# Normalising the attention output: psO copied out before the reciprocal, and the reciprocal moved by a DMA

## The chip, the cores and the metric

The kernel runs on the 8 cores of one Trainium2 chip. Every core computes one of the 8 sequences, by the same program, and the cores exchange nothing. The metric is the device time of the slowest core, in microseconds. All rows below are those of core 3, the slowest one of the profiled execution.

## The reference

One transformer layer over x of [8, 2048, 1024] in float32: causal attention of 16 heads of width 64 on the normalised x, with a residual, and then a gated feed-forward part on the normalised sum, with a residual.

```python
h = layernorm(x)
q, k, v = rope(split_heads(h @ Wq)), rope(split_heads(h @ Wk)), split_heads(h @ Wv)
attn = softmax(where(causal, q @ k.T * 64 ** -0.5, -inf))
x = x + merge_heads(attn @ v) @ Wo + bo
h = layernorm(x)                      # hp: h one position earlier
r = sigmoid((mu_r * h + (1 - mu_r) * hp) @ W_r.T)
k = square(relu((mu_k * h + (1 - mu_k) * hp) @ W_k.T))
out = x + r * (k @ W_v.T)
```

## The kernel before

The program is one list of operations, each with an engine, the tokens it reads and the tokens it writes. From the tokens the helper class `_Sched` (L37) works out which earlier operations each one waits for, by one counting semaphore for each engine and one for each engine's DMA queue. Each engine then executes its own operations strictly in the order of the list. A DMA waits for the one before it on its queue too (L115 to L119), unless both are of one batch. The DMA queue "sync" is SP's, the queue "sp" is POOL's.

The stages: layer norm of x with a transpose into h1t (to 88 us), the projections of Q and K with the rotation (to 215), the projection of V and the attention (216 to 656), the product with Wo and the second layer norm (658 to 756), and the feed-forward part (to the end).

The attention takes the heads in pairs: p = 0 to 7, one head on partitions 0 to 63 of qt and kt, the other on 64 to 127. Each pair has four units ic = 0 to 3, of 512 query columns each (L457). Unit ic walks over the 4ic + 4 blocks J of 128 keys that causality leaves, so the units have 4, 8, 12 and 16 steps. In a step TensorE computes the scores of both heads (L474 and L479, into psA or psB, with the mask added by L485 and L488 on the diagonal blocks), ScalarE takes exp (L491, into one of three tiles er), and TensorE accumulates in psO: L505 adds V times er to partitions 0 to 63, L513 adds ones times er, the row sums, to partitions 64 to 127. Columns 0 to 511 are the first head's, columns 512 to 1023 the second's. The even units accumulate in psO0, the odd ones in psO1. Each has a token for each half: `otokA` and `otokB`.

A unit's tail (`tail_maker`, L522) is what VectorE does when all steps of a unit are done: the reciprocal of the 64x1024 row sums into denl (L523), the product for the first head into ao (L526, called nmA), the product for the second head into aotmp (L531, nmB), and an SP DMA of 64 KB that brings aotmp to partitions 64 to 127 of ao (L534, amv). ao, which shares its memory with h1t, is what the Wo stage reads.

The loop of L555 writes the order: the scores run one step ahead of the product with V, and the tail of a unit is put in after the first scores of the next one, ahead of its first product with V. A unit's first L505 waits for the tail of the unit two before it, which used the same psO. In pair 0 each new unit is preceded by the projection of V for four more token tiles (`emit_vproj`, L344: TensorE L352 into the four halves of psA and psB, VectorE L359 evacuates them), and these evacuations stand ahead of the preceding unit's tail on VectorE.

Wo is loaded by POOL once the scores of pair 3 are done (L571), followed on the same queue by 14 tiles of x of 512 KB each (L577). The last two tiles of x go into the memory of the tiles er and are loaded after the last step. The Wo stage (L598) waits for the last amv.

Of the kernel before, what the change touches and what calls it, by code (L numbers as in the profile page):

```python
# [158 lines left out]
def _build_nc(upto=99, taps=()):  # L159
# [37 lines left out]
    B_ao = sb("ao", [128, 16384], BF16, 86016)  # L197
# [29 lines left out]
    DENl = sb("denl", [128, 1024], F32, 218048)  # L227
    qrawK = sb("qrawK", [128, 2048], BF16, 222144)
    aotmp = sb("aotmp", [128, 1024], BF16, 226240)
# [12 lines left out]
    A = s.add  # L242
# [29 lines left out]
    for cb in range(CC):  # L272
        e, f, rd, wr = wload(WA, 1024 * cb, wq_t, 128 * cb, f"waq{cb}")
        A("sp", f, reads=rd, writes=wr, is_dma=True, name=f"ld_wq{cb}", batch="wq")
    for cb in range(CC):
        e, f, rd, wr = wload(WB, 1024 * cb, wk_t, 128 * cb, f"wbk{cb}")
# [89 lines left out]
    for j in range(TT):  # L366
# [3 lines left out]
          writes=[f"xring{j % 4}"], is_dma=True, name=f"ldx{j}", batch=f"x{j // 2}")  # L370
# [56 lines left out]
    for cb in range(CC):  # L427
        A("sp", (lambda cb=cb: lambda g: g.dma_start(WA[:, 1024 * cb:1024 * (cb + 1)],
                                                     wv_t[128 * cb:128 * (cb + 1), :]))(),
          reads=[], writes=[f"wav{cb}", f"waq{cb}"], is_dma=True, name=f"ld_wv{cb}", batch="wv")  # L430
# [29 lines left out]
    def unit_ctx(p, ic):  # L460
            psO = psO0 if ic % 2 == 0 else psO1
            otokA = "ps4" if ic % 2 == 0 else "ps6"
            otokB = "ps5" if ic % 2 == 0 else "ps7"
            nJ = 4 * ic + 4

            def emit_scores(J, slot):
                i0 = max(512 * ic, 128 * J)
                w = 512 * (ic + 1) - i0
                sreg = psA if J % 2 == 0 else psB
                stokA = "ps0" if J % 2 == 0 else "ps2"  # L470
                stokB = "ps1" if J % 2 == 0 else "ps3"
                es, etok = Er[slot], f"E{slot}"
                diag = J >= 4 * ic
                A("pe", (lambda p=p, J=J, i0=i0, w=w, sreg=sreg, diag=diag: lambda t: t.matmul(  # L474
                    sreg[:, 0:w], D_kt[0:64, 2048 * p + 128 * J:2048 * p + 128 * J + 128],
                    C_qt[0:64, 2048 * p + i0:2048 * p + i0 + w], start=True, stop=not diag,
                    tile_position=(0, 0)))(),
                  reads=[f"kt_p{p}", f"qt_p{p}"], writes=[stokA, f"qt_r{p}", f"kt_r{p}"], name=f"sA{p}_{ic}_{J}")
                A("pe", (lambda p=p, J=J, i0=i0, w=w, sreg=sreg, diag=diag: lambda t: t.matmul(  # L479
                    sreg[:, 512:512 + w], D_kt[64:128, 2048 * p + 128 * J:2048 * p + 128 * J + 128],  # L480
                    C_qt[64:128, 2048 * p + i0:2048 * p + i0 + w], start=True, stop=not diag,
                    tile_position=(64, 0)))(),
                  reads=[f"kt_p{p}", f"qt_p{p}"], writes=[stokB, f"qt_r{p}", f"kt_r{p}"], name=f"sB{p}_{ic}_{J}")
                if diag:
                    A("pe", (lambda sreg=sreg: lambda t: t.matmul(  # L485
                        sreg[:, 0:128], idb[:, :], mnegb[:, :], start=False, stop=True))(),
                      reads=["idb", "mnegb"], writes=[stokA], name=f"mA{p}_{ic}_{J}")
                    A("pe", (lambda sreg=sreg: lambda t: t.matmul(  # L488
                        sreg[:, 512:640], idb[:, :], mnegb[:, :], start=False, stop=True))(),
                      reads=["idb", "mnegb"], writes=[stokB], name=f"mB{p}_{ic}_{J}")  # L490
                A("act", (lambda sreg=sreg, es=es, w=w: lambda sc: sc.activation(  # L491
                    es[:, :].rearrange("p (a b) -> p a b", a=2)[:, :, 0:w],
                    sreg[:, :].rearrange("p (a b) -> p a b", a=2)[:, :, 0:w],
                    AF.Exp, scale=0.125))(),
                  reads=[stokA, stokB], writes=[etok, stokA, stokB], name=f"ex{p}_{ic}_{J}")

            def emit_pv(J, slot):
                i0 = max(512 * ic, 128 * J)
                w = 512 * (ic + 1) - i0
                rel = i0 - 512 * ic  # L500
                es, etok = Er[slot], f"E{slot}"
                for hb, otok, ecol, ocol in ((0, otokA, 0, 0), (1, otokB, 512, 512)):
                    h = 2 * p + hb
                    A("pe", (lambda J=J, h=h, w=w, rel=rel, es=es, ecol=ecol, ocol=ocol, psO=psO, nJ=nJ:
                             lambda t: t.matmul(  # L505
                        psO[0:64, ocol + rel:ocol + rel + w],
                        E_v[:, 1024 * J + 64 * h:1024 * J + 64 * h + 64],
                        es[:, ecol:ecol + w],
                        start=(J == 0), stop=(J == nJ - 1), tile_position=(0, 0),
                        skip_group_check=True))(),  # L510
                      reads=[etok, f"vsb{J}"], writes=[otok], name=f"pv{p}_{ic}_{J}_{hb}")
                    A("pe", (lambda J=J, w=w, rel=rel, es=es, ecol=ecol, ocol=ocol, psO=psO, nJ=nJ:
                             lambda t: t.matmul(  # L513
                        psO[64:128, ocol + rel:ocol + rel + w],
                        ones128[:, 0:64],
                        es[:, ecol:ecol + w],
                        start=(J == 0), stop=(J == nJ - 1), tile_position=(0, 64),
                        skip_group_check=True))(),
                      reads=[etok, "ones"], writes=[otok], name=f"pd{p}_{ic}_{J}_{hb}")


            def tail_maker(p=p, ic=ic, psO=psO, otokA=otokA, otokB=otokB):  # L522
                A("dve", (lambda psO=psO: lambda v: v.reciprocal(  # L523
                    DENl[64:128, :], psO[64:128, :]))(),
                  reads=[otokA, otokB], writes=["denl"], name=f"rcp{p}_{ic}")
                A("dve", (lambda p=p, ic=ic, psO=psO: lambda v: v.tensor_mul(  # L526
                    B_ao[0:64, 2048 * p + 512 * ic:2048 * p + 512 * ic + 512],
                    psO[0:64, 0:512], DENl[64:128, 0:512]))(),
                  reads=[otokA, "denl", "h1t"], writes=["ao"], name=f"nmA{p}_{ic}")
                at_sl = slice(512 * (ic % 2), 512 * (ic % 2) + 512)  # L530
                A("dve", (lambda p=p, ic=ic, psO=psO, at_sl=at_sl: lambda v: v.tensor_mul(  # L531
                    aotmp[0:64, at_sl], psO[0:64, 512:1024], DENl[64:128, 512:1024]))(),
                  reads=[otokB, "denl"], writes=[f"aot{ic % 2}", otokB], name=f"nmB{p}_{ic}")
                A("sync", (lambda p=p, ic=ic, at_sl=at_sl: lambda sy: sy.dma_start(  # L534
                    B_ao[64:128, 2048 * p + 512 * ic:2048 * p + 512 * ic + 512],
                    aotmp[0:64, at_sl]))(),
                  reads=[f"aot{ic % 2}"], writes=["ao"], is_dma=True, name=f"amv{p}_{ic}")
            return emit_scores, emit_pv, tail_maker
# [31 lines left out]
    for cb in range(CC):  # L570
        A("sp", (lambda cb=cb: lambda g: g.dma_start(Wo_sb[:, 1024 * cb:1024 * (cb + 1)],  # L571
                                                     wo_t[128 * cb:128 * (cb + 1), :]))(),
          reads=["kt_r0", "kt_r1", "kt_r2", "kt_r3"],
          writes=[f"wo{cb}"], is_dma=True, name=f"ld_wo{cb}", batch="wo")

    for j in list(range(0, 4)) + list(range(6, 16)) + [4, 5]:
        A("sp", (lambda j=j: lambda g: g.dma_start(Ax[:, 1024 * j:1024 * (j + 1)],  # L577
                                                   x_t[128 * j:128 * (j + 1), :]))(),
          reads=[], writes=[f"xt{j}"] + x_deps[j], is_dma=True, name=f"ldx2_{j}",
# [4 lines left out]
      reads=["bo32"], writes=["bo32"], is_dma=True, name="bo_ld")  # L584
    A("dve", lambda v: v.tensor_copy(boHi[0:64, :], bo32[0:64, :]),
      reads=["bo32"], writes=["bohi"], name="bo_hi")
    A("dve", lambda v: v.tensor_sub(boLo[0:64, :], bo32[0:64, :], boHi[0:64, :]),
      reads=["bo32", "bohi"], writes=["bolo"], name="bo_lo")
# [4 lines left out]
    for n, tt in enumerate(tt_order):  # L593
        for half in range(2):
            slot = halfbanks[(n * 2 + half) % 4]
            ptok = f"ps{(n * 2 + half) % 4}"
            for cb in range(CC):
# [5 lines left out]
                  reads=["ao", f"wo{cb}"], writes=[ptok, "wodone"], name=f"wo{tt}_{half}_{cb}")  # L603
# [3 lines left out]
              reads=["bohi", "ones"], writes=[ptok], name=f"bh{tt}_{half}")  # L607
# [3 lines left out]
              reads=["bolo", "ones"], writes=[ptok], name=f"bl{tt}_{half}")  # L611
# [4 lines left out]
              reads=[ptok, f"xt{tt}", f"res{tt}"], writes=[f"res{tt}", ptok], name=f"ra{tt}_{half}")  # L616
# [28 lines left out]
    for cb in range(CC):  # L645
# [3 lines left out]
          reads=["wodone"],  # L649
          writes=[f"wr{cb}"], is_dma=True, name=f"ld_wr{cb}", batch="wr")  # L650
# [39 lines left out]
    for tt in [12, 13, 14, 15, 8, 9, 10, 11, 4, 5, 6, 7, 0, 1, 2, 3]:  # L690
        for half in range(2):
            slot = halfbanks[(tt * 2 + half) % 8]
            ptok = f"ps{(tt * 2 + half) % 8}"
            for cb in range(CC):
# [5 lines left out]
                  reads=[f"xr_t{tt // 4}", f"wr{cb}"], writes=[ptok, "rmdone"], name=f"rm{tt}_{half}_{cb}")  # L700
# [3 lines left out]
              reads=[ptok, "vsb"], writes=[f"rs_t{tt}", ptok], name=f"sg{tt}_{half}")  # L704
# [3 lines left out]
    for cb in range(CC):  # L708
# [3 lines left out]
          reads=["rmdone"],  # L712
          writes=[f"wkf{cb}"], is_dma=True, name=f"ld_wkt{cb}", batch="wkt")
# [39 lines left out]
    for cb in range(CC):  # L753
# [3 lines left out]
          reads=["xkr0", "xkr1"] + [f"xr_t{t}" for t in range(4)],  # L757
          writes=[f"wvf{cb}"], is_dma=True, name=f"ld_wvt{cb}", batch="wvt")

    n_store = 0  # L760
    for tt in [12, 13, 14, 15, 8, 9, 10, 11, 4, 5, 6, 7, 0, 1, 2, 3]:
        for half in range(2):
            slot = halfbanks[(tt * 2 + half) % 8]
            ptok = f"ps{(tt * 2 + half) % 8}"
            for dk in range(CC):
# [5 lines left out]
                  reads=[f"ka_t{tt // 4}", f"wvf{dk}"], writes=[ptok], name=f"vm{tt}_{half}_{dk}")  # L771
# [3 lines left out]
              reads=[ptok, f"rs_t{tt}"], writes=["p9scr", ptok], name=f"v1{tt}_{half}")  # L775
# [81 lines left out]
```

How the kernel before makes its waits and increments, by code:

```python
            def body(eng):  # L129
                for op in per_eng[eng_name]:
                    for pkey in sorted(op.resolved_waits):
                        val = op.resolved_waits[pkey]
                        if marks.get((eng_name, pkey), 0) >= val:
                            continue
                        marks[(eng_name, pkey)] = val
                        eng.wait_ge(sems[pkey], val)
                    ins = op.fn(eng)
                    if op.is_dma:
                        ins.then_inc(sems[self.semkey(op)], 16)
                    elif op.inc_needed:
                        ins.then_inc(sems[self.semkey(op)], 1)
# [661 lines left out]
        def syb(sy):  # L803
            bodies["sync"](sy)
            for k in sorted(qtot):
                sy.wait_ge(sems[k], qtot[k])
```

## Time and profile before

| | us |
|---|---|
| median of 2 runs | 969.9 (969.31 to 970.49) |
| the profiled execution, its own time | 971.39 |
| its span, slowest core | 969.8 |
| spans of the 8 cores | 958.3 to 969.8 |
| busy in the span: PE, DVE, ACT | 754.9, 579.2, 435.9 |
| mean granted TensorE clock, core 3 | 0.941 |

The span runs from the first to the last instruction on the core; the execution's own time has something around it. PE is TensorE's matmul, PEld its weight load, DVE is VectorE, ACT ScalarE, POOL GpSimd. A busy share is an average over stages with different limits.

### The profile page before, as it was taken

What the parts mean: (1) busy time and instruction counts of PE and PEld (TensorE: products, weight loads), DVE (VectorE), ACT (ScalarE), POOL (GpSimd) and SP (SyncE); (2) the same over time, 40 slices, a digit from 0 to 9 for tenths busy, and PEclk for the clock granted to TensorE, in tenths of its full rate; (3) what the DMA queues carried; (4) which work ended last, traced back from release to release, by engine and by line L of the source; (5) the groups of instructions that cost most, each with busy time, mean ns of one, the idle gap of its engine ahead of it and who ended that gap; (6) DMA issues with size and microseconds to landing.
All of it is one profiled execution on the core that took longest, in us unless ns stands there. A gap on an engine that the chain in (4) does not pass through costs nothing.

```text
span 969.8 us, 12954 instructions; the slowest of 8 cores (958.3 to 969.8 us)
## 1 busy us (share of the span) xinstructions
PE 754.9 (78%) x4288; PEld 299.5 (31%) x4288; DVE 579.2 (60%) x740; ACT 435.9 (45%) x580; POOL 42.9 (4%) x83
## 2 busy tenths in 40 slices
PE   0115999969998787878787877768998499297998
PEld 0113444423332222222222222212343244043443
DVE  3554443563545848484848575754777886056587
ACT  3444332311246676767676767651444233022200
POOL 3100001000000000001300000000001000101000
PEclk9999999999999898989998999996999699598999
DMA  7960337320000000000860000010000500600633
GB/s 172 190 174 31 77 77 130 88 65 1 4 4 3 9 5 9 4 9 14 164 228 9 4 9 4 9 32 18 1 1 8 80 1 1 87 1 4 127 152 152
DMA packets 21121, 52.30 MB, mean 54 GB/s; under 512 B 3360, under 2 KB 5408, under 8 KB 21056
## 3 DMA queue, kind: packets, MB, share of 16 engines
q0 software_dynamic: 10816, 24.20, 13.4%
q1 hardware_dynamic: 8704, 23.07, 7.7%
q10 hardware_dynamic: 1536, 4.20, 1.9%
q8 instruction: 36, 0.59, 0.2%
q14 instruction: 29, 0.24, 0.1%
HBM read 47.26 MB, written 8.39 MB: 57 GB/s over the span
## 4 chain that ended last, share of the span: by engine, by line
PE 54%; DVE 15%; ACT 14%; DMA 11%; issue 5%; POOL 1%; DVEq 0%; ACTq 0%; SPq 0%; POOLq 0%
ACT er L491 11%; PE psO L505 11%; DVE denl L523 5%; DMA xri<-x 5%; PE psO L402 5%; PE psA L474 5%; PE psO L766 3%; PE psA L352 3%; PE psB L598 3%; PE psB L352 2%; PE psA L402 2%; PE psA L598 2%; DMA swp<-qraw 2%; PE psB L402 2%; DVE xr L669 2%
## 5 line engine op out<-in xcount | busy, mean ns | idle before, releaser
L523 DVE RECIPROCAL denl<-psO 64x1024 f32<-64x1024 f32 x32 | 209.9, 6560 | 119.3 <-PE psO L513 118.5
L505 PE MATMUL psO<-er,vsb 128*64 128x512 bf16 (+3 forms) x640 | 181.7, 364 | 74.8 <-ACT er L491 49.9
L491 ACT ACTIVATE er<-psA 128x1024 bf16<-128x1024 f32 (+1 forms) x160 | 150.2, 939 | 132.0 <-PE psA L479 96.2
L513 PE MATMUL psO<-er,ones 128*64 128x512 bf16 (+3 forms) x640 | 187.4, 374 | 0.0
L491 ACT ACTIVATE er<-psB 128x1024 bf16<-128x1024 f32 (+2 forms) x160 | 136.0, 850 | 11.9 <-PE psB L488 8.0
L505 PEld LDWEIGHTS psO<-er,vsb 128*64 128x64 bf16 x640 | 47.7, 108 | 144.6 <-issue 138.1
L320 PE MATMUL psO<-idb,hs 128*128 128x128 bf16 x128 | 16.2, 307 | 72.4 <-ACT hs L305 70.0
L479 PE MATMUL psA<-qt,kt 64*128 64x512 bf16 (+1 forms) x160 | 61.0, 381 | 0.0
L474 PE MATMUL psA<-qt,kt 64*128 64x512 bf16 (+1 forms) x160 | 61.0, 381 | 0.0
L418 DVE TENSOR_TENSOR swp<-swp,sinb 128x2048 bf16<-128x2048 bf16 x16 | 19.6, 1225 | 67.2 <-DMA swp<-qraw 57.7
L479 PE MATMUL psB<-qt,kt 64*128 64x512 bf16 (+2 forms) x160 | 56.4, 353 | 0.3
L474 PE MATMUL psB<-qt,kt 64*128 64x512 bf16 (+2 forms) x160 | 56.5, 353 | 0.0
L737 DVE TENSOR_TENSOR ka<-ka 128x512 bf16<-128x512 bf16 x32 | 13.6, 425 | 56.7 <-ACT ka L733 56.6
L513 PEld LDWEIGHTS psO<-er,ones 128*64 128x64 bf16 x640 | 46.9, 109 | 0.0
L598 PE MATMUL psA<-wosb,ao 128*128 128x512 bf16 x128 | 33.7, 411 | 10.3 <-DMA ao<-aotmp 10.3
L721 PE MATMUL psA<-xkr,wktsb 128*128 128x512 bf16 x64 | 18.7, 458 | 25.1 <-DMA wktsb<-wkt 18.9
L352 PE MATMUL psA<-wa,h1t 128*128 128x512 bf16 x128 | 31.0, 399 | 8.0 <-DVE vsb L359 8.0
L410 ACT CAST qraw<-psO 128x512 bf16<-128x512 f32 x32 | 18.8, 586 | 38.8 <-PE psO L402 17.1
L286 ACT ACTIVATE vsb<-ax 128x1024 bf16<-128x1024 f32 x16 | 16.9, 1057 | 42.8 <-DVE ax L612 42.8
L282 DVE TENSOR_REDUCE stats<-xri 128x1 f32<-128x1024 f32 x16 | 19.4, 1213 | 27.6 <-DMA xri<-x 27.6
L320 PEld LDWEIGHTS psO<-idb,hs 128*128 128x128 bf16 x128 | 12.4, 138 | 75.9 <-issue 75.9
L474 PEld LDWEIGHTS psA<-qt,kt 64*128 64x128 bf16 x160 | 14.9, 93 | 60.1 <-issue 60.1
(129 smaller groups left out, 1192.3 us busy)
## 6 DMA issues: line engine op xcount, KB each, us to landing
xri<-x SPq DMA_DIRECT2D x16, 512.0 KB, 6.4
ax<-x POOLq DMA_DIRECT2D x16, 512.0 KB, 12.9
out<-ax SPq DMA_DIRECT2D x16, 512.0 KB, 2.6
swp<-qraw ACTq DMA_DIRECT2D x24, 128.0 KB, 2.4
swp<-qraw SPq DMA_DIRECT2D x24, 128.0 KB, 2.7
wa<-wq POOLq DMA_DIRECT2D x8, 256.0 KB, 12.9
wb<-wk POOLq DMA_DIRECT2D x8, 256.0 KB, 13.1
wa<-wv POOLq DMA_DIRECT2D x8, 256.0 KB, 11.2
```

The source lines that it names most:

```text
L320: return t.matmul(o, h_ap_fn(k), idb[:, :], start=(k4 == 0), stop=(k4 == 3), is_transpose=True)
L352: return t.matmul(ps[:, o:o + 512], B_h1t[:, 2048 * cb + 128 * tt:2048 * cb + 128 * tt + 128], WA[:, 1024 * cb + 512 * half:1024 * cb + 51 ...
L402: return t.matmul(ps[:, o:o + 512], Wsb[:, 1024 * cb + 128 * co:1024 * cb + 128 * co + 128], B_h1t[:, 2048 * cb + 512 * tch:2048 * cb + 51 ...
L418: A("dve", (lambda sw=sw: lambda v: v.tensor_mul(sw[:, :], sw[:, :], sinb[:, :]))(), reads=stoks + ["sinb"], writes=stoks, name=f"{tag}r1_ ...
L474: A("pe", (lambda p=p, J=J, i0=i0, w=w, sreg=sreg, diag=diag: lambda t: t.matmul(sreg[:, 0:w], D_kt[0:64, 2048 * p + 128 * J:2048 * p + 12 ...
L479: A("pe", (lambda p=p, J=J, i0=i0, w=w, sreg=sreg, diag=diag: lambda t: t.matmul(sreg[:, 512:512 + w], D_kt[64:128, 2048 * p + 128 * J:204 ...
L491: A("act", (lambda sreg=sreg, es=es, w=w: lambda sc: sc.activation(es[:, :].rearrange("p (a b) -> p a b", a=2)[:, :, 0:w], sreg[:, :].rear ...
L505: lambda t: t.matmul(psO[0:64, ocol + rel:ocol + rel + w], E_v[:, 1024 * J + 64 * h:1024 * J + 64 * h + 64], es[:, ecol:ecol + w], start=( ...
L513: lambda t: t.matmul(psO[64:128, ocol + rel:ocol + rel + w], ones128[:, 0:64], es[:, ecol:ecol + w], start=(J == 0), stop=(J == nJ - 1), t ...
L523: A("dve", (lambda psO=psO: lambda v: v.reciprocal(DENl[64:128, :], psO[64:128, :]))(), reads=[otokA, otokB], writes=["denl"], name=f"rcp{ ...
L598: A("pe", (lambda tt=tt, half=half, cb=cb, slot=slot: lambda t: t.matmul(slot[0][:, slot[1]:slot[1] + 512], B_ao[:, 2048 * cb + 128 * tt:2 ...
L766: A("pe", (lambda tt=tt, half=half, dk=dk, slot=slot: lambda t: t.matmul(slot[0][:, slot[1]:slot[1] + 512], B_ka[:, 2048 * dk + 128 * tt:2 ...
```

## The change

In the tail of a unit, the row sums, the first head's part of psO and the second head's part are first copied to SBUF by VectorE: denl in float32, ao and aotmp in bfloat16. The reciprocal then reads and writes denl in SBUF, partitions 64 to 127. A new SP DMA (dmv) moves the 64x1024 reciprocals, 256 KB of float32, to partitions 0 to 63 of denl, and the two products are done in place in SBUF, with both operands on partitions 0 to 63. The DMA of aotmp into ao follows as before. Nothing else is changed.

```diff
             def tail_maker(p=p, ic=ic, psO=psO, otokA=otokA, otokB=otokB):
-                A("dve", (lambda psO=psO: lambda v: v.reciprocal(
+                at_sl = slice(512 * (ic % 2), 512 * (ic % 2) + 512)
+                A("dve", (lambda psO=psO: lambda v: v.tensor_copy(
                     DENl[64:128, :], psO[64:128, :]))(),
-                  reads=[otokA, otokB], writes=["denl"], name=f"rcp{p}_{ic}")
-                A("dve", (lambda p=p, ic=ic, psO=psO: lambda v: v.tensor_mul(
+                  reads=[otokA, otokB], writes=["denl", otokA, otokB], name=f"cpD{p}_{ic}")
+                A("dve", (lambda p=p, ic=ic, psO=psO: lambda v: v.tensor_copy(
                     B_ao[0:64, 2048 * p + 512 * ic:2048 * p + 512 * ic + 512],
-                    psO[0:64, 0:512], DENl[64:128, 0:512]))(),
-                  reads=[otokA, "denl", "h1t"], writes=["ao"], name=f"nmA{p}_{ic}")
-                at_sl = slice(512 * (ic % 2), 512 * (ic % 2) + 512)
-                A("dve", (lambda p=p, ic=ic, psO=psO, at_sl=at_sl: lambda v: v.tensor_mul(
-                    aotmp[0:64, at_sl], psO[0:64, 512:1024], DENl[64:128, 512:1024]))(),
-                  reads=[otokB, "denl"], writes=[f"aot{ic % 2}", otokB], name=f"nmB{p}_{ic}")
+                    psO[0:64, 0:512]))(),
+                  reads=[otokA, "h1t"], writes=["aoU", otokA], name=f"cpOA{p}_{ic}")
+                A("dve", (lambda psO=psO, at_sl=at_sl: lambda v: v.tensor_copy(
+                    aotmp[0:64, at_sl], psO[0:64, 512:1024]))(),
+                  reads=[otokB], writes=[f"aot{ic % 2}", otokB], name=f"cpOB{p}_{ic}")
+                A("dve", lambda v: v.reciprocal(DENl[64:128, :], DENl[64:128, :]),
+                  reads=["denl"], writes=["denl"], name=f"rcp{p}_{ic}")
+                A("sync", lambda sy: sy.dma_start(DENl[0:64, :], DENl[64:128, :]),
+                  reads=["denl"], writes=["denl2"], is_dma=True, name=f"dmv{p}_{ic}")
+                A("dve", (lambda p=p, ic=ic: lambda v: v.tensor_mul(
+                    B_ao[0:64, 2048 * p + 512 * ic:2048 * p + 512 * ic + 512],
+                    B_ao[0:64, 2048 * p + 512 * ic:2048 * p + 512 * ic + 512],
+                    DENl[0:64, 0:512]))(),
+                  reads=["aoU", "denl2"], writes=["ao"], name=f"nmA{p}_{ic}")
+                A("dve", (lambda ic=ic, at_sl=at_sl: lambda v: v.tensor_mul(
+                    aotmp[0:64, at_sl], aotmp[0:64, at_sl], DENl[0:64, 512:1024]))(),
+                  reads=[f"aot{ic % 2}", "denl2"], writes=[f"aot{ic % 2}"], name=f"nmB{p}_{ic}")
```

## Rows read from the trace of the kernel before

**Rows 1.** The page, part 4: the chain that ended last, by line.
```profile
ACT er L491 11%; PE psO L505 11%; DVE denl L523 5%; DMA xri<-x 5%; PE psO L402 5%; PE psA L474 5%; PE psO L766 3%; PE psA L352 3%; PE psB L598 3%; PE psB L352 2%; PE psA L402 2%; PE psA L598 2%; DMA swp<-qraw 2%; PE psB L402 2%; DVE xr L669 2%
```

**Rows 2.** Stretches of pairs 1 and 4: busy us by engine, clock, DMA share, GB/s.
```profile
312.00:361.00 49.00, 39.60 (x282) 13.00 (x282) 31.36 (x12) 34.80 (x42) 0.00 (x0) 0.93 0.03 7
457.50:505.00 47.50, 37.71 (x274) 12.52 (x272) 31.36 (x12) 34.40 (x41) 10.61 (x21) 0.96 0.81 206
```

**Rows 3.** VectorE in order of time, pair 1: start, us; idle before, releaser.
```profile
312.92 6.56 DVE L523 RECIPROCAL denl<-psO 64x1024 f32<-64x1024 f32 x1 [9.63 <-PE psO L513]
319.65 0.68 DVE L526 TENSOR_TENSOR ao<-psO,denl 64x512 bf16<-64x512 f32 x1 [0.17 <-DVE denl L523]
320.26 0.67 DVE L531 TENSOR_TENSOR aotmp<-psO,denl 64x512 bf16<-64x512 f32 x1
321.10 6.56 DVE L523 RECIPROCAL denl<-psO 64x1024 f32<-64x1024 f32 x1 [0.17 <-PE psO L513]
...
330.01 6.56 DVE L523 RECIPROCAL denl<-psO 64x1024 f32<-64x1024 f32 x1 [0.90 <-PE psO L513]
...
343.18 6.56 DVE L523 RECIPROCAL denl<-psO 64x1024 f32<-64x1024 f32 x1 [5.16 <-PE psO L513]
...
361.06 6.56 DVE L523 RECIPROCAL denl<-psO 64x1024 f32<-64x1024 f32 x1 [9.49 <-PE psO L513]
```

**Rows 4.** TensorE in order of time around the start of unit 1, pair 1.
```profile
313.91 0.38 PE L505 MATMUL psO<-er,vsb 128*64 128x512 bf16 x1 [0.65 <-ACT er L491]
...
316.54 0.22 PE L505 MATMUL psO<-er,vsb 128*64 128x128 bf16 x1
...
320.48 0.61 PE L505 MATMUL psO<-er,vsb 128*64 128x512 bf16 x1 [3.39 <-DVE ao L526]
```

**Rows 5.** Waits of TensorE for VectorE (us, times, longest), and all reciprocals.
```profile
PE psO L505 <- DVE ao L526: 23.7, 7, 3.4
...
L523 DVE RECIPROCAL denl<-psO x32: 6560/6560/6562, 245.5 to 648.3; 64x1024 f32<-64x1024 f32 x32
```

**Rows 6.** Short stretches, columns as in rows 2: the granted clock.
```profile
320.00:321.00 1.00, 0.52 (x2) 0.16 (x2) 0.93 (x2) 0.00 (x0) 0.00 (x0) 0.50 0.00 0
325.00:326.00 1.00, 1.00 (x6) 0.32 (x6) 1.00 (x1) 0.25 (x1) 0.00 (x0) 0.50 0.00 0
326.00:327.00 1.00, 1.00 (x10) 0.27 (x8) 1.00 (x1) 0.78 (x1) 0.00 (x0) 0.86 0.00 0
656.00:658.00 2.00, 0.00 (x0) 0.00 (x0) 1.24 (x2) 0.00 (x0) 0.00 (x0) 0.50 0.14 32
```

**Rows 7.** The chain in order of time in pair 0: start us, us, what.
```profile
246.28 0.38 PE psO L505
...
253.25 3.56 PE psA L352 x16
256.81 3.45 PE psB L352 x16
```

**Rows 8.** VectorE's groups by shape: busy, mean ns, idle before and releasers.
```profile
L776 DVE TENSOR_TENSOR ax<-ax,dscr 128x512 f32<-128x512 f32 x32 | 22.2, 692 | 3.3
L526 DVE TENSOR_TENSOR ao<-psO,denl 64x512 bf16<-64x512 f32 x32 | 21.8, 683 | 6.9 <-DVE denl L523 5.6 <-DMA ao<-aotmp 1.2
...
L359 DVE CAST vsb<-psA 128x512 bf16<-128x512 f32 x16 | 11.1, 691 | 26.9 <-PE psA L352 26.7 <-DVE vsb L359 0.2
...
L587 DVE TENSOR_TENSOR bolo<-bo,bohi 64x1024 bf16<-64x1024 f32 x1 | 1.2, 1216 | 0.1
...
L585 DVE CAST bohi<-bo 64x1024 bf16<-64x1024 f32 x1 | 0.7, 685 | 2.4 <-DMA bo<-bo 2.4
```

**Rows 9.** The chain in order of time at the end of the attention.
```profile
648.32 6.57 DVE denl L523
...
655.73 0.61 DVE aotmp L531
...
656.46 1.90 DMA ao<-aotmp
658.36 0.14 issue
658.50 1.86 PE psA L598 x4
```

**Rows 10.** DMA issues: KB each, median us from issue to landing.
```profile
out<-ax SPq DMA_DIRECT2D x16, 512.0 KB, 2.6
swp<-qraw ACTq DMA_DIRECT2D x24, 128.0 KB, 2.4
...
ao<-aotmp SPq DMA_DIRECT2D x32, 64.0 KB, 1.9
```

**Rows 11.** Landing of the single L534 DMA issued in 464:467, 480:484 and 490:496.
```profile
DMA to landing us min/median/max: 7.7/7.7/7.7
...
DMA to landing us min/median/max: 7.0/7.0/7.0
...
DMA to landing us min/median/max: 5.5/5.5/5.5
```

## The prediction

> **What bounds the kernel now.** I read the page's chain first [rows 1]: the two attention lines L491 (exp) and L505 (the product with V) are the longest terms, and the reciprocal at L523 is third with 5%. Then the stretches [rows 2]: one pair of heads takes 47.5 to 48.5 us from the second pair on, TensorE is busy about 38 us of it and VectorE 31.4, so no engine is full on average; the granted clock is 0.93 to 0.96. The question is which wait ends last where a unit begins. VectorE's order of time shows a tail [rows 3]: the reciprocal at 312.92, nmA at 319.65, nmB at 320.26, next reciprocal at 321.10, 8.18 us. The reciprocals of units 0, 1, 2 and 3 of the pair start at 321.10, 330.01, 343.18 and 361.06. That of unit 0 is late: its last product was issued at 316.54 [rows 4], and VectorE was still in the tail of the preceding unit 3. TensorE meanwhile stands before unit 1, because psO1 is read by that same tail: its product at 320.48 came 3.39 us late, released by nmA (L526) [rows 4]. This happens once per pair: 7 times, 23.7 us in all [rows 5]. After the idle time the granted clock is at 0.50, which is the 1.2 GHz level, and returns to 1.00 (2.4 GHz) at about 326 [rows 6]: unit 1 then needs 9.5 us (320.48 to 330.01), where the same eight steps of pair 0 took 7.0 us at full clock (246.28 to 253.25) [rows 7].
>
> **What the change takes away.** psO is freed once three copies have read it, and not after the reciprocal. Count from the tail's start. cpD, 64x1024 from PSUM: 128x512 casts from PSUM take 0.69 us, 64x1024 at one element per cycle takes 1.22 (L587) [rows 8], so 1.22 (the ends are 0.69 and 1.23). cpOA waits for it through a semaphore, 0.17 as between L523 and L526 [rows 3], and takes 0.69, as L359 [rows 8]. So psO's first half is free at 2.1 us, where it was 7.4. In the pair read above the stall of 3.4 us would shrink to the wait for exp, about 0.5 to 1 us (the step without a stall at 313.91 shows 0.65 [rows 4]), and the slow clock's 2.5 us would go too. About 2.7 + 2.5 = 5.2 us per pair, 36 us over seven, if nothing else became late.
>
> **What it adds: a longer tail on VectorE, one instruction stream.** VectorE takes its instructions in order, and nmA now waits for the DMA dmv. Behind nmA on VectorE stand nmB and the next unit's cpD, cpOA and cpOB, and for these TensorE waits. So the DMA's landing time counts as VectorE time. The length D of a tail, start to start:
> cpD 1.22, gap 0.17, cpOA 0.61 (start to start, as nmA to nmB [rows 3]), cpOB 0.69, together 2.69. Then the reciprocal 6.56, now from SBUF: 6.4 ns per element is far over one cycle, so the division sets it and not the source, and I keep it: 9.25. Issue and landing of dmv: 0.12 from nmB's end to the DMA and 0.14 from its landing to the waiting engine, both from the end of the attention stage [rows 9], around a landing time X. Then nmA 0.61 and nmB 0.67. D = 9.25 + 0.26 + X + 1.28 = 10.8 + X. In the SBUF form of nmA a 128x512 tensor_tensor of float32 takes 0.69 (L776) [rows 8], so it is no cheaper and no dearer.
> X is for 256 KB in 64 pieces of 4 KB. Rows: 64 KB in pieces of 1 KB land in 1.9, 128 KB in pieces of 4 KB in 2.4 (with a second such transfer beside it), 512 KB of 128 pieces in 2.6 [rows 10]. I take 2.6, the upper neighbour. The ends are 1.9 and 3.4 (0.5 more for each 64 KB, as between the first two). D is 13.4, from 12.7 to 14.2.
>
> **Does D bind?** Four tails take 4 x 13.4 = 53.6 us, and a pair now takes 48. The other limit is TensorE's: tail 0 cannot start before tail 3's end (D after it), unit 2 needs psO0 from tail 0 (2.1 later), then units 2 and 3 run 13.2 + 17.9 = 31.1 us [rows 3], plus up to 2.5 for a slow clock. That is D + 33.2 to D + 35.7, 49.1 at most with D at 13.4. It passes 4D only below D = 11.9. So from the tail of unit 3 of pair 0 (312.92), with VectorE idle before it, every later tail finds its unit ready and they follow one another without a pause. Check at the tightest place: unit 3 starts 2.1 after tail 1's start, or when unit 2 ends, and its own tail comes 2D = 26.8 after tail 1's start; 2.1 + 17.9 + 2.5 = 22.5. It is ready. Inside pair 0 the TensorE work of the V projection (14 us per four tiles [rows 7]) hides the longer tails: tail 0, started at 245.5 [rows 5], would end at 258.9. The evacuation of 0.69 behind it would be done at 259.6, and TensorE wants it only when its four psA/psB halves are used up, at 260.3 (253.25 + 3.56 + 3.45). That cover is 0.7 us: with X above 3.3 it is gone, and TensorE waits there once by what X is longer.
>
> **The sum.** Tails start at 312.92 for pair 0 and at 648.32 for pair 7 [rows 3, 9]: 28 intervals in 335.4 us, 11.98 each. With D at 13.4 this is 28 x 1.42 = +39.8. At the end nothing hides the tail: today TensorE restarts 10.2 us after the last tail's start (658.50), 2.2 us of it from nmB's end [rows 9]; it becomes 13.4 + 2.2 = 15.6, +5.4. The clock is at 0.5 before that restart already [rows 6], so no clock is lost there.
> The loads of Wo and of x run under pair 4 today (457.5 to 505), with the DMA engines 0.81 busy in that stretch [rows 2], and the 64 KB transfers issued inside it landed in 7.7, 7.0 and 5.5 us instead of 1.9 [rows 11], 4.8 more on average. Only once did it cost VectorE anything (1.2 us [rows 8]), since nmA only waits for the amv of a unit before. Now each dmv stands in VectorE's own stream: 4.8 more, some 0.7 for its fourfold bytes, 5.5. 0.81 of 47.5 us is 38 us, and with tails of 17 to 19 us a little over 2 such transfers fall into it: +12, from 0 to 22.
> Together 39.8 + 5.4 + 12 = +57. The profiled execution took 971.4 us (its span 969.8), which gives 1028.6; the median of the runs shown is 1.5 us below the profiled one, so the forecast is 1027.
>
> **Two rules beside the rows.** On X: with 64 pieces the transfer reads partitions 64 to 127 and writes 0 to 63. The Trainium skill, page "SBUF — State Buffer", section "Door 1: The DMA port swizzle", says that such a range reaches only 8 of the 16 ports, so 64 partitions move no faster than 32. With that page's 218 GB/s and 2 us fixed cost an estimate would be X = 3.2, D = 14.0 and a time of about 1044. By that estimate 128 KB would take 2.6, and the trace has 2.4 [rows 10], so I stay with the rows.
> On the reciprocal: the cast from SBUF of 64x1024 took 0.69, the same as half as many elements from PSUM [rows 8]. So an operation with one source, both ends in SBUF, can run at two elements per cycle here, and the reciprocal now is such an operation. That is rival B below. The Trainium skill, "VectorE: DVE Perf Modes", section "Mode 2×_2P — use both read ports for one tensor", states this as a rule for copies and tensor_scalar, float32 too.
>
> **Rivals.**
> A. The freed psO decides, and VectorE doesn't. For: the stall of 23.7 us and the slow clock behind it are real [rows 5, 6]. It needs D + 33.2 at or below the 42.8 that a pair would take without the stall, so D up to 9.6; the reciprocal, three copies and two products alone make 10.5. Time 971.4 - 36 + 5 - 1.5 = 939. Chance 0.02.
> B. The reciprocal from SBUF takes half, 3.4. Then D is 10.2, TensorE's limit holds, D + 35.7 = 45.9 per pair, 7 x 2.1 = 15 gained, 2.2 lost at the end and 3 at the loads: less the 1.5 us to the median, about 960. Against: the operation is bound by its division at 6.4 ns per element, not by its reads. Chance 0.06.
> C. The tail has the steps that I list, but the small terms fall low: X 1.9, copies overlapped, no load hit by a dmv. D = 12.4, 28 x 0.42 + 4.4 = 16, about 986. Chance 0.07.
> D. Contention is worse: several dmv take 10 us and more, or X is 3.4. 1050 to 1060. Chance 0.12.
> E. The change doesn't release psO early (the release would still be counted at the last VectorE instruction). The tokens say otherwise: cpOA is the last to name psO's first half. It would move the time little anyway, since D holds the tails; 0.01, about 1030.
> The forecast has 0.72.
>
> **The range.** From 1000 (D 12.7, loads +5) to 1052 (D 13.9, loads +22). A measurement of this kernel tells about 2% from no change, 19 us. Faster by more: A, 0.02. Within it: B and nearly all of C, 0.10. Slower: 0.88.
>
> **What would show it.** In the profile after: from 313 us to the end of the attention VectorE has no idle time but the wait of nmA for the DMA, 2.6 to 3 us, some 30 times; the wait of the reciprocal for TensorE (118.5 us now) all but goes; the tails start 13.4 us apart in every pair, whatever the unit's length; TensorE's wait for VectorE grows and is named by cpOA or cpOB; a pair takes 53 to 54 us with more slices at a low clock; psO's release at 2.1 us after the tail's start. Wrong if the reciprocal's mean leaves 6.56, if X is not between 2.4 and 3, or if the reciprocal still waits for TensorE in the long units: then TensorE sets the pace and the pair stays under 50 us.

## The result, and the profile after

| | before | after |
|---|---|---|
| median of all runs | 972.52 us (10 runs) | 1031.96 us (11 runs) |
| ratio | | 1.061, 95% interval 1.059 to 1.063 |
| the profiled execution | 971.39 us | 1032.68 us |
| spans of the 8 cores | 958.3 to 969.8 us | 1017.7 to 1031.1 us |
| mean granted clock, slowest core | 0.941 | 0.907 |

The kernel became 6% slower; 1027 was forecast, with a range of 1000 to 1052. In some executions the cores of one die run at a lower clock and longer; ratios, intervals and the two times given for e4 leave those out, medians don't. The rows of after are those of core 4, its slowest.

VectorE in order of time, from the tail of the last unit of pair 0 to that of unit 1 of pair 1 (start us, us, instruction, idle before it and releaser); it answers to [rows 3]:

```profile
317.10 1.23 DVE L524 COPY denl<-psO 64x1024 f32<-64x1024 f32 x1 [4.08 <-PE psO L513]
318.43 0.68 DVE L527 CAST ao<-psO 64x512 bf16<-64x512 f32 x1
319.04 0.67 DVE L531 CAST aotmp<-psO 64x512 bf16<-64x512 f32 x1
319.75 6.55 DVE L534 RECIPROCAL denl<-denl 64x1024 f32<-64x1024 f32 x1
329.38 0.68 DVE L538 TENSOR_TENSOR ao<-ao,denl 64x512 bf16<-64x512 bf16 x1 [3.08 <-DMA denl<-denl]
329.99 0.68 DVE L543 TENSOR_TENSOR aotmp<-aotmp,denl 64x512 bf16<-64x512 bf16 x1
330.70 1.23 DVE L524 COPY denl<-psO 64x1024 f32<-64x1024 f32 x1
...
344.47 1.23 DVE L524 COPY denl<-psO 64x1024 f32<-64x1024 f32 x1
```

One tail is 13.60 us from start to start. The second cpD has no bracket: VectorE goes straight from nmB to the next unit's copy. The only idle time of note inside is the 3.08 us for which nmA stands for dmv. Two groups of VectorE show the same over all 32 tails (busy us, mean ns, idle before and what ended it):

```profile
L534 DVE RECIPROCAL denl<-denl 64x1024 f32<-64x1024 f32 x32 | 209.6, 6550 | 1.0
L524 DVE COPY denl<-psO 64x1024 f32<-64x1024 f32 x32 | 39.3, 1228 | 5.1 <-PE psO L513 4.1
```

VectorE once waited 118.5 us for TensorE ahead of its tails; now it is 4.1 us, once, before pair 0's last tail. The waits (engine, line, releaser: us in total, times, longest) tell who waits in its place:

```profile
DVE ao L538 <- DMA denl<-denl: 110.9, 32, 9.1
...
PE psO L505 <- DVE ao L527: 67.7, 13, 10.3
```

TensorE's wait for psO has grown from 23.7 us in 7 times [rows 5] to 67.7 in 13, though psO is free 2.0 us into the tail: what it waits for is not the copy but the whole tail that stands ahead of it on VectorE. The transfers (KB each, median us to landing), as in [rows 10]:

```profile
denl<-denl SPq DMA_DIRECT2D x32, 256.0 KB, 2.9
```

The stretches of pairs 1 and 2 and of the loads (columns as in [rows 2]):

```profile
317.00:371.70 54.70, 42.45 (x304) 14.07 (x302) 41.40 (x25) 39.10 (x46) 0.00 (x0) 0.94 0.11 24
371.70:426.00 54.30, 41.38 (x272) 12.82 (x272) 40.90 (x24) 34.75 (x40) 0.00 (x0) 0.87 0.12 25
480.00:540.00 60.00, 37.22 (x244) 11.39 (x244) 39.39 (x24) 31.11 (x35) 7.32 (x14) 0.80 0.57 169
```

A pair takes 54 to 55 us, the two under which Wo and x are loaded 59.5 and 60.4. VectorE is "busy" 41 of 54, and yet it is the bound: four waits for dmv of 3.1 us make 12 of the missing 13. TensorE's granted clock is 0.94 and 0.87 in the first two stretches, where it was 0.93. That is not what lengthens a pair, since VectorE's tails follow without a pause. Under the loads, nmA's waits are those of the transfer (VectorE in order of time):

```profile
484.63 0.68 DVE L538 TENSOR_TENSOR ao<-ao,denl 64x512 bf16<-64x512 bf16 x1 [8.16 <-DMA denl<-denl]
504.23 0.69 DVE L538 TENSOR_TENSOR ao<-ao,denl 64x512 bf16<-64x512 bf16 x1 [9.09 <-DMA denl<-denl]
517.86 0.69 DVE L538 TENSOR_TENSOR ao<-ao,denl 64x512 bf16<-64x512 bf16 x1 [3.13 <-DMA denl<-denl]
```

And the chain at the end of the attention (start us, us, what), which answers to [rows 9]:

```profile
709.84 1.24 DVE denl L524
...
712.48 6.56 DVE denl L534
...
719.16 2.86 DMA denl<-denl
...
723.52 1.92 DMA ao<-aotmp
725.44 0.14 issue
725.58 3.57 PE psA L610 x8
```

The 61.3 us between the two spans are these: pair 0's last tail starts at 317.10 instead of 312.92, +4.2; the 28 intervals from there to the last tail take 392.7 instead of 335.4, +57.3; the last tail to TensorE's restart 15.7 instead of 10.2, +5.6; from the restart to the end 305.5 instead of 311.3, -5.8.

The +4.2 is not the change's. It is there at the first tail of all (249.68 instead of 245.50), before any changed instruction has run, and over the eight cores pair 0's last tail starts at 312.7 before and 312.5 after in the median. The -5.8 is more than a choice of core: from the restart on, the eight cores of before take 304.8 to 311.3 us (median 308.7), those of after 300.3 to 305.5 (median 302.6). So the later restart is made up for behind it: from the last tail's start to the end of its span the median core takes 318.8 us before and 318.5 after. No run shows by what.

### The profile page after: what moved, and what is told of

Same layout as the page of the kernel before. It is cut to its first block, busy times and chain, and to the rows that moved or that the text cites. A ratio compares the mean times of both kernels' runs of the same rounds, so it can differ in the third digit from the quotient of the medians.

```text
span 1031.1 us, 13211 instructions; the slowest of 8 cores (1017.7 to 1031.1 us)
## 1 busy us (share of the span) xinstructions
PE 776.2 (75%) x4288; PEld 302.1 (29%) x4288; DVE 659.3 (64%) x836; ACT 437.9 (42%) x580; POOL 42.9 (4%) x83
## 3 DMA queue, kind: packets, MB, share of 16 engines
q0 software_dynamic: 10816, 24.20, 11.5%
## 4 chain that ended last, share of the span: by engine, by line
PE 45%; DVE 29%; DMA 14%; ACT 6%; issue 5%; DVEq 0%; POOL 0%; SPq 0%; ACTq 0%; POOLq 0%
DVE denl L534 13%; DMA denl<-denl 7%; PE psO L402 5%; DMA xri<-x 5%; PE psO L505 5%; ACT er L491 4%; DVE denl L524 3%; PE psA L402 3%; PE psA L352 3%; PE psO L778 3%; PE psB L402 3%; PE psB L610 3%; PE psA L610 2%; PE psB L352 2%; PE psO L733 2%
## 5 line engine op out<-in xcount | busy, mean ns | idle before, releaser
L505 PE MATMUL psO<-er,vsb 128*64 128x512 bf16 (+3 forms) x640 | 195.9, 386 | 107.9 <-DVE ao L527 67.7
L534 DVE RECIPROCAL denl<-denl 64x1024 f32<-64x1024 f32 x32 | 209.6, 6550 | 1.0
L513 PE MATMUL psO<-er,ones 128*64 128x512 bf16 (+3 forms) x640 | 201.3, 396 | 0.0
L505 PEld LDWEIGHTS psO<-er,vsb 128*64 128x64 bf16 x640 | 49.1, 112 | 185.2 <-issue 178.5
L538 DVE TENSOR_TENSOR ao<-ao,denl 64x512 bf16<-64x512 bf16 x32 | 21.9, 684 | 110.9 <-DMA denl<-denl 110.9
L479 PE MATMUL psA<-qt,kt 64*128 64x512 bf16 (+1 forms) x160 | 64.0, 400 | 0.0
L474 PE MATMUL psA<-qt,kt 64*128 64x512 bf16 (+1 forms) x160 | 64.0, 400 | 0.0
L479 PE MATMUL psB<-qt,kt 64*128 64x512 bf16 (+2 forms) x160 | 58.0, 362 | 0.4
L474 PE MATMUL psB<-qt,kt 64*128 64x512 bf16 (+2 forms) x160 | 58.0, 362 | 0.0
L524 DVE COPY denl<-psO 64x1024 f32<-64x1024 f32 x32 | 39.3, 1228 | 5.1 <-PE psO L513 4.1
L352 PE MATMUL psA<-wa,h1t 128*128 128x512 bf16 x128 | 33.3, 420 | 8.3 <-DVE vsb L359 8.3
## 6 DMA issues: line engine op xcount, KB each, us to landing
wb<-wk POOLq DMA_DIRECT2D x8, 256.0 KB, 13.5
```

What stands on the lines that cost most here:

```text
L352: return t.matmul(ps[:, o:o + 512], B_h1t[:, 2048 * cb + 128 * tt:2048 * cb + 128 * tt + 128], WA[:, 1024 * cb + 512 * half:1024 * cb + 51 ...
L505: lambda t: t.matmul(psO[0:64, ocol + rel:ocol + rel + w], E_v[:, 1024 * J + 64 * h:1024 * J + 64 * h + 64], es[:, ecol:ecol + w], start=( ...
L513: lambda t: t.matmul(psO[64:128, ocol + rel:ocol + rel + w], ones128[:, 0:64], es[:, ecol:ecol + w], start=(J == 0), stop=(J == nJ - 1), t ...
L524: A("dve", (lambda psO=psO: lambda v: v.tensor_copy(DENl[64:128, :], psO[64:128, :]))(), reads=[otokA, otokB], writes=["denl", otokA, otok ...
L534: A("dve", lambda v: v.reciprocal(DENl[64:128, :], DENl[64:128, :]), reads=["denl"], writes=["denl"], name=f"rcp{p}_{ic}")
```

## The experiments

**e1, the copy does what the transfer did.** cpD writes the row sums to partitions 0 to 63, so nothing has to be moved.

```diff
-                    DENl[64:128, :], psO[64:128, :]))(),
+                    DENl[0:64, :], psO[64:128, :]))(),
...
-                A("dve", lambda v: v.reciprocal(DENl[64:128, :], DENl[64:128, :]),
+                A("dve", lambda v: v.reciprocal(DENl[0:64, :], DENl[0:64, :]),
...
-                A("sync", lambda sy: sy.dma_start(DENl[0:64, :], DENl[64:128, :]),
-                  reads=["denl"], writes=["denl2"], is_dma=True, name=f"dmv{p}_{ic}")
...
```

> The changed kernel, but cpD writes the row sums straight to partitions 0 to 63 of denl, so dmv is not needed and nmA waits for no DMA. Theory (VectorE's stream of tails sets the pace, and the landing time of dmv stands in it): D falls from 13.6 to 13.6 - 3.1 = 10.5 us. Then four tails take 42 us, TensorE's chain D + 33.2 = 43.7 us per pair governs against 48 in the kernel before, the stall before unit 1 is gone, and the loads no longer touch a tail: 7 x 4.3 = 30 us less than before, 2.3 more at the end, about 943 us, ratio 0.971. Rival 1 (the slow clock stays, D + 35.7 = 46.2 per pair): about 961. Rival 2 (the copies and TensorE's lower clock cost the time, not the wait for the DMA): stays above 1010.

Measured 945.1 us, ratio 0.973 (0.971 to 0.975). Tails that follow one another are 10.7 us apart, and from the last tail of pair 0 (318.06) to that of pair 7 (624.72) it is 306.7 us, 43.8 per pair. Two stretches of about a pair, at full clock:

```profile
315.00:359.00 44.00, 36.53 (x276) 12.43 (x272) 39.50 (x22) 34.66 (x41) 0.00 (x0) 1.00 0.03 6
359.00:402.50 43.50, 36.04 (x272) 12.42 (x272) 40.76 (x25) 34.13 (x41) 0.00 (x0) 1.00 0.03 7
```

Granted 1.00 in both. TensorE's waits for VectorE ahead of L505 are gone from the list. So with the transfer and its wait out of the stream the change is a gain of 2.7% instead of a loss of 6.1%. VectorE is busy 40 of 44 us here and only just no longer the bound: three of a pair's four intervals are 10.7, and the fourth, ahead of unit 3's tail, is 11.5 to 11.9. Both rivals fall.

**e2, the transfer kept, its wait put behind other work.** With a second denl buffer, nmA, nmB and amv of a unit are emitted behind the three copies of the next unit, which is what `flush_norm` does.

```diff
+                flush_norm()
                 A("dve", lambda v: v.reciprocal(DN[64:128, :], DN[64:128, :]),
                   reads=[dt], writes=[dt], name=f"rcp{p}_{ic}")
                 A("sync", lambda sy: sy.dma_start(DN[0:64, :], DN[64:128, :]),
                   reads=[dt], writes=[dt2], is_dma=True, name=f"dmv{p}_{ic}")
...
+                pend_norm.append(norm)
```

> The changed kernel with dmv kept, but nmA, nmB and amv of a unit are put behind the three copies of the next unit, with two denl buffers, so VectorE no longer stands idle for a transfer unless tails follow at once. Theory (the wait in the stream is the cost, the transfer itself is not): D 10.5 to 11, a pair 44 to 45, 25 us less than before, 7 more at the end since both transfers of the last unit are exposed, about 5 at the loads: about 958 us, ratio 0.985. Rival (the 256 KB transfers cost by their traffic or by SP's queue): 1000 or more.

Measured 965.6 us, ratio 0.994 (0.992 to 0.996): the loss is gone with the transfer still there, but the gain is 8 us less than expected. VectorE under the loads:

```profile
435.66 0.68 DVE L541 TENSOR_TENSOR ao<-ao,denm 64x512 bf16<-64x512 bf16 x1 [0.45 <-DMA denm<-denm]
...
452.86 0.69 DVE L541 TENSOR_TENSOR ao<-ao,denl 64x512 bf16<-64x512 bf16 x1 [6.62 <-DMA denl<-denl]
...
466.55 0.68 DVE L541 TENSOR_TENSOR ao<-ao,denm 64x512 bf16<-64x512 bf16 x1 [3.19 <-DMA denm<-denm]
```

In a quiet stretch the deferred wait is 0.45 us, where it was 3.08. Under the loads three copies of 2.6 us don't hide a landing of 9, and the four tails from 432.6 take 58.2 us against 43.8 in a quiet pair, 14 more where I had counted 5. These 9 us are about the size of the miss.

**e3, the transfer alone.** The kernel before, and one more 256 KB transfer per unit, within a scratch tile, that no instruction of an engine waits for.

```diff
+                A("sync", lambda sy: sy.dma_start(DENx[0:64, :], DENx[64:128, :]),
+                  reads=["denx"], writes=["deny"], is_dma=True, name=f"dmx{p}_{ic}")
```

> The kernel before with one more SP DMA per unit, 256 KB from partitions 64 to 127 to 0 to 63 of a scratch tile, as dmv, behind amv; no instruction of any engine waits for it. Theory (the transfer costs only where VectorE stands for it): 972 us, plus 0 to 6 in the pair under which the loads run, since there amv has to queue behind it on SP and nmA waits for the amv of the unit before; ratio 1.00 to 1.006. Rival (traffic and SP's queue were part of the loss): 10 us or more, ratio above 1.01.

Measured 971.2 us, ratio 0.9995 (0.998 to 1.001). The median landing time is 2.9 us, as in the changed kernel, and all of them together cost nothing that these runs can tell. The traffic is free; standing for it is not.

**e4, a longer stream alone.** The kernel before, with a reciprocal of 64x850 on a scratch tile behind nmB.

```diff
+                A("dve", lambda v: v.reciprocal(DENx[0:64, 0:850], DENx[0:64, 0:850]),
+                  reads=["denx"], writes=["denx"], name=f"pad{p}_{ic}")
```

> The kernel before with one more VectorE instruction behind nmB in each tail, a reciprocal of 64x850 on a scratch tile that nobody reads; psO is freed as in the kernel before, 8 us into the tail, and no transfer is added. Theory (only the length of VectorE's stream counts): D = 8.2 + 5.6 = 13.8, tails follow without a pause from pair 0's last on, 28 x 1.8 = 51 us, and up to 3 at the end where the bias work comes later: about 1025 us, ratio 1.055. Rival 1 (the wait for the DMA or the traffic is what costs, VectorE has room on average): 972 to 985. Rival 2 (the early release of psO had saved something in the changed kernel): clearly above 1035.

Measured 1018.9 and 1021.1 us beside 970.2 to 973.0 for the kernel before: a ratio near 1.05, for which two runs give no interval. VectorE in order of time:

```profile
326.59 6.56 DVE L525 RECIPROCAL denl<-psO 64x1024 f32<-64x1024 f32 x1
333.32 0.68 DVE L528 TENSOR_TENSOR ao<-psO,denl 64x512 bf16<-64x512 f32 x1 [0.17 <-DVE denl L525]
333.93 0.67 DVE L533 TENSOR_TENSOR aotmp<-psO,denl 64x512 bf16<-64x512 f32 x1
334.64 5.46 DVE L536 RECIPROCAL denx<-denx 64x850 f32<-64x850 f32 x1
340.12 6.56 DVE L525 RECIPROCAL denl<-psO 64x1024 f32<-64x1024 f32 x1
```

The period is 13.53 us in all 28 intervals, 378.9 us against 335.4. No transfer, no early release, and the same picture as in the changed kernel at the same D: TensorE waits 61.1 us for VectorE ahead of its products with V, in 14 times, where it was 67.7 in 13. Here VectorE is busy 53 of a pair's 54 us; in the changed kernel it is 41 of 54, and the pace is the same. The load term is missing (every interval is 13.53, also under the loads). That term, 11.9, and 28 times 0.07 make the 13.8 us by which the changed kernel's 28 intervals are longer. psO is freed 7.4 us into each tail here and 2.0 in the changed kernel, and it makes no difference at this D. What I had set too high was the pad, 5.46 us and not 5.6.

**e5, the changed kernel without 14 loads of x.** GpSimd fills these tiles with zeros, so the residual is left out of the output there.

```diff
+        if j in (4, 5):
             A("sp", (lambda j=j: lambda g: g.dma_start(Ax[:, 1024 * j:1024 * (j + 1)],
...
+        else:
+            A("sp", (lambda j=j: lambda g: g.memset(Ax[:, 1024 * j:1024 * (j + 1)], 0.0))(),
+              reads=[], writes=[f"xt{j}"] + x_deps[j], name=f"zx2_{j}")
```

> The changed kernel without 14 of the 16 loads of x for the residual: GpSimd fills these tiles with zeros instead, so the residual is missing from the output for them. Only the loads of Wo remain beside the tails. Theory (each dmv issued under the loads lands late, and VectorE stands for it): of the two long intervals between tails, 18.7 and 19.6 us instead of 13.6, the second goes, the first stays: 6 us less than the changed kernel, about 1025 us, with 28 intervals of 13.6 and one of 18.7. Rival (the long intervals come from Wo's loads alone, or from something else in that pair): no change, 1031.

Measured 1026.3 us, ratio 1.056 (1.054 to 1.058) against the changed kernel's 1.061 (1.059 to 1.063): about 5 us less, uncertain by some 3. The trace is clearer: the 28 intervals take 387.2 us instead of 392.7, and the long ones are 18.93 and 13.62 where they were 18.67 and 19.59. In its VectorE order one long wait is left, that of the tail over which Wo is loaded; the next one is short again:

```profile
464.35 0.68 DVE L538 TENSOR_TENSOR ao<-ao,denl 64x512 bf16<-64x512 bf16 x1 [3.12 <-DMA denl<-denl]
483.28 0.68 DVE L538 TENSOR_TENSOR ao<-ao,denl 64x512 bf16<-64x512 bf16 x1 [8.43 <-DMA denl<-denl]
496.90 0.68 DVE L538 TENSOR_TENSOR ao<-ao,denl 64x512 bf16<-64x512 bf16 x1 [3.12 <-DMA denl<-denl]
```

**e6, no transfer at all.** The row sums of the two heads go to the two halves of the partitions, the numerators straight to both halves of ao, and reciprocal and product handle 128 partitions at once; aotmp and amv go too.

```diff
+                A("dve", lambda v: v.tensor_copy(DENl[0:64, 0:512], psO[64:128, 0:512]),
...
+                A("dve", lambda v: v.tensor_copy(B_ao[0:64, aoc], psO[0:64, 0:512]),
...
+                A("dve", lambda v: v.tensor_copy(DENl[64:128, 0:512], psO[64:128, 512:1024]),
...
+                A("dve", lambda v: v.tensor_copy(B_ao[64:128, aoc], psO[0:64, 512:1024]),
...
+                A("dve", lambda v: v.reciprocal(DENl[:, 0:512], DENl[:, 0:512]),
...
+                A("dve", lambda v: v.tensor_mul(B_ao[:, aoc], B_ao[:, aoc], DENl[:, 0:512]),
...
```

> No transfer at all: the first head's row sums are copied to partitions 0 to 63 of denl, the second head's to 64 to 127, the numerators straight to both halves of ao, then one reciprocal of 128x512 and one product of 128x512 in place. Theory (D decides until TensorE's chain does): four copies 2.8, reciprocal 512 x 6.4 ns = 3.4, product 0.7: D = 6.9. TensorE's chain alone sets a pair, 42.8 us, the full 36 us of the stall and its slow clock come back, and the end is 3 shorter: about 932 us, ratio 0.96. Rival (the stall before unit 1 is taken by the wait for exp, and the slow clock stays): 945 to 960.

Measured 942.9 us, ratio 0.970 (0.968 to 0.972), the fastest of all, but 11 us above what I expected. D is 7.35 us (the reciprocal of 128x512 takes 3.35, about half as long for the same number of results). A stretch of one pair, and TensorE's first products of units 0 and 1:

```profile
359.40:403.20 43.80, 36.32 (x274) 12.42 (x272) 27.20 (x24) 34.42 (x41) 0.00 (x0) 1.00 0.00 1
```

```profile
316.76 0.38 PE L505 MATMUL psO<-er,vsb 128*64 128x512 bf16 x1 [0.65 <-ACT er L491]
320.79 0.38 PE L505 MATMUL psO<-er,vsb 128*64 128x512 bf16 x1 [0.85 <-ACT er L491]
```

The pair is 43.8 us, exactly as in e1, though D went from 10.7 to 7.35: below 10.7 a shorter tail buys nothing inside a pair. What is left at unit 1's start is the wait for exp. A pair costs TensorE and ScalarE 43.8 us together at full clock, where I had put 42.8, and seven pairs make 7 of the 11 us. The end of the attention is 2.8 us shorter than before (7.4 us from the last tail's start to the restart), as expected. Of the other 4 us, 2.8 lie ahead of the last tail of pair 0 (at 315.7 here, 312.9 before), and they are there at the first tail already (248.34 against 245.50), before anything that differs has run.

**e7, e6 with psO freed late.** The numerators are not copied; the two products read psO. The edit is shown against e6.

```diff
-                A("dve", lambda v: v.tensor_copy(B_ao[0:64, aoc], psO[0:64, 0:512]),
...
+                A("dve", lambda v: v.tensor_mul(B_ao[0:64, aoc], psO[0:64, 0:512], DENl[0:64, 0:512]),
...
+                A("dve", lambda v: v.tensor_mul(B_ao[64:128, aoc], psO[0:64, 512:1024], DENl[64:128, 0:512]),
...
```

> As e6, without the copies of the numerators: two copies of row sums (one for each half of denl), a reciprocal of 128x512, then the two products read psO, the second written straight to partitions 64 to 127 of ao. psO is freed late again, some 5.5 us (first half) into the tail, where e6 frees it at 3, the kernel before at 7.4. D = 1.4 + 3.4 + 1.3 and gaps = 6.3. Theory (TensorE's own chain is what is left once D is short; the early release is worth little then): the wait of unit 1's first product for psO ends about when its exp does, a pair 43.7 to 44.3, the end 4 shorter than before: 938 to 944 us, ratio 0.965 to 0.971. Rival (the early release is what gave the gain of e1 and e6): the stall and the slow clock stay in part, 46 to 48 a pair, 955 to 965.

Measured 957.3 us, ratio 0.985 (0.983 to 0.987): here the rival was right, and my theory, with 938 to 944, was wrong. D is 6.5 us, the shortest of all, and yet it is 14 us slower than e6; a pair takes 45.9 (321.0 us for seven). TensorE at unit 1, and the clock behind it (columns as above):

```profile
320.60 0.38 PE L505 MATMUL psO<-er,vsb 128*64 128x512 bf16 x1 [1.57 <-ACT er L491]
321.38 0.52 PE L505 MATMUL psO<-er,vsb 128*64 128x512 bf16 x1 [0.38 <-DVE ao L532]
```

```profile
320.00:322.00 2.00, 1.02 (x6) 0.38 (x6) 1.83 (x4) 0.53 (x1) 0.00 (x0) 0.87 0.01 4
322.00:324.00 2.00, 2.00 (x10) 0.33 (x10) 1.90 (x2) 1.02 (x1) 0.00 (x0) 0.50 0.00 0
324.00:326.00 2.00, 2.00 (x14) 0.50 (x12) 2.00 (x1) 1.36 (x2) 0.00 (x0) 0.77 0.00 0
```

The profile names exp as the releaser of the product at 320.60, but exp's step is of the kind that costs 0.85 in e6; the 1.57 us end 0.16 after nmA's end (319.76 + 0.68). A second wait of 0.38 for nmB follows. That is about 1.1 us of extra idle time beside e6, and then the granted clock is at the 1.2 GHz level for some 3 us, where it is 1.00 throughout in e6's stretch above. The early release is thus worth 14 us once D is short, and nothing where D is 13.5.

## Why the prediction was right

The mechanism held: psO is freed early and TensorE gains nothing by it, since VectorE's tails, with a DMA's landing time inside each, follow one another without a pause and set the pace.

- D was put at 13.4 and is 13.60. What was off is X, the landing of dmv: 2.9 us and not 2.6. The other terms nearly hold (the three copies 2.65 for 2.69, the idle time around the landing 0.22 for 0.26, the two products 1.32 for 1.28). 28 intervals of 13.60 against 11.98 make +45.4 where +39.8 was forecast.
- The reciprocal from SBUF takes 6.55, so rival B is out: its time does not go by the source. e6 shows that it goes by the elements per partition.
- By the Trainium skill, "SBUF — State Buffer", section "Door 1: The DMA port swizzle", with that page's fixed cost of 2 us, the estimate for X was 3.2. The trace's 2.9 lies midway between it and my 2.6. That 256 KB over 64 partitions need more than the 2.6 of 512 KB over all 128 fits its rule and speaks against my choice of the neighbouring row.
- The load term was +12; the two long intervals (18.67 and 19.59) are 11.1 above two of 13.60, the other intervals 0.9 together, and e5 makes the second of the two short again by leaving the loads of x out.
- The end was +5.4, and TensorE's restart comes 5.6 later, but this does not reach the total, as said above.
- Pair 0's cover held: its first three intervals between tails are 22.51, 27.27 and 17.64 us, where they were 22.50, 27.27 and 17.65, and the evacuations behind the first tail (from 263.22) let the V projection run on without a wait.
- That D binds is shown by e4, which has the same pace with no transfer and no early release, by e1 and e2, in which the loss goes with the wait, and by e3, where the transfer alone costs nothing.

The other limit, TensorE's chain of D + 33.2 to D + 35.7 per pair, is shown by no kernel. At e1's D of 10.7 it gives 43.9, and 43.8 was measured, but that is a coincidence: TensorE waits for VectorE nowhere ahead of L505 in e1, and e6 takes the same 43.8 with D = 7.35, for which the chain gives 40.6. What takes over below D = 10.95 (a quarter of 43.8) is what TensorE and ScalarE need for a pair by themselves. The forecast did not need the chain, since four tails of 13.4 are longer than either end of it.

Mis-sized, without harm to the forecast: the value of the stall. I had 5.2 us per pair, 36 in all; e1 and e6, without it, show 47.9 - 43.8 = 4.1 per pair, 29 in all. The larger part of the difference is a misreading of the clock's cost. The 7.0 us of pair 0's unit 1, to 253.25, hold seven of its eight steps, since its last product comes behind the V projection; the 9.5 of pair 1 hold all eight and the wait up to the tail. The rows of before, TensorE in order of time: the seventh and the eighth step of unit 1 in pair 0, then the eighth in pair 1.

```profile
252.95 0.27 PE L505 MATMUL psO<-er,vsb 128*64 128x256 bf16 x1
...
267.51 0.22 PE L505 MATMUL psO<-er,vsb 128*64 128x128 bf16 x1
...
329.64 0.22 PE L505 MATMUL psO<-er,vsb 128*64 128x128 bf16 x1
```

In pair 1 unit 1's products go from 320.48 to 329.64 before, 9.2 us, and in e6 at full clock from 320.79 to 328.09, 7.3. So the low clock costs 1.9 us and not 2.5. From unit 0's last product to unit 1's first it is 3.9 us before and 1.4 in e6, which gives back 2.5 of the 2.7. Together that is 4.4 in this pair, and the mean over seven is 4.1. The time of rival A, 939, was therefore too low by 7 us.

Some of the closeness of 1027 is luck: the sum of D left 28 x 0.2 = 5.6 us out, and the end's 5.4, which it had in, was made up for behind the restart. The two nearly cancel.

What stays open: what makes up for the later restart. No kernel was run for it.

## What to carry to other kernels

Before copying a buffer out early, add up the whole stream of the engine that copies: a DMA's landing time counts in full if the next instruction on that engine waits for it, and the busy share (here 76% in a pair) doesn't show it. The release is worth something only while that stream, repeated as often as the work comes round, is shorter than the work of the engine that it releases (the changed kernel against e4, where it is worth nothing, and e6 against e7, where it is worth 14 us). If data has to change partitions on its way out of PSUM, let the copy that is needed anyway write them to the right place, and use all 128 partitions for an operation whose time goes by the elements per partition.

## What the runs showed of the hardware

- A VectorE copy moved partitions 64 to 127 of PSUM to 0 to 63 of SBUF, and 0 to 63 to 64 to 127, at the price of a straight one: 0.68 to 0.69 us for 64x512 and 1.23 for 64x1024.
- The reciprocal takes 6.55 us for 64x1024, 5.46 for 64x850 and 3.35 for 128x512, and it is the same from PSUM (6.56) and from SBUF: 6.4 to 6.5 ns for each element of a partition.
- 32 transfers of 256 KB between partitions, beside everything else, cost nothing (ratio 0.9995, 0.998 to 1.001), and yet under loads that keep the DMA engines busy one of them lands up to 8.9 us after its issue instead of 2.9.
- A small extra wait can cost more than its length: in e7 TensorE stood 1.1 us longer than in e6 before unit 1, the granted clock fell to 0.50 for some 3 us, and the pair was 2.1 us longer on average.
